# Local attention and feed-forward: columns turned from unshifted rows, norms batch by batch, groups turned singly

## The reference, cut to what matters

```python
def shift_token(t):
    t1, t2 = jnp.split(t, 2, axis=-1)
    t2 = jnp.pad(t2, ((0, 0), (1, 0), (0, 0)))[:, :-1]
    return jnp.concatenate([t1, t2], axis=-1)

def _layer(x, wqkv, qs, ksc, wo, lg, lb, w1, b1, w2, b2):
    h = shift_token(x)
    q, k, v = jnp.split(h @ wqkv, 3, axis=-1)
    q, k = l2norm(q) * qs, l2norm(k) * ksc
    q, k = rotary_xpos(q, k)
    x = x + local_attention(q, k, v) @ wo
    h = shift_token(x)
    h = (h - mu) / jnp.sqrt(var + 1e-05) * lg + lb
    a, g = jnp.split(h @ w1 + b1, 2, axis=-1)
    return x + (a * gelu(g)) @ w2 + b2

for l in range(2): y = _layer(y, ...)     # y = layernorm(x) at first
x = x + y
```

## Time and profile before

| | us |
|---|---|
| median of 3 runs | 4430.23 (4429.78 to 4431.81) |
| the profiled execution | 4434.21 |
| its span in the profile | 4432.4 |
| TensorE busy | 3285.2 (74%) |
| VectorE busy | 3454.3 (78%) |
| ScalarE busy | 2186.3 (49%) |
| GpSimd busy | 2297.1 (52%) |

### The profile page before, as it was taken

One profiled execution on the slowest core, in us unless ns is written; L12 is line 12 of the kernel. 1 busy time (PEld: TensorE's weight loads), 2 busy tenths in 40 slices (PEclk: granted clock), 3 DMA queues, 4 the chain that ended last, 5 costly groups with the idle time before them and its releaser, 6 DMA issues. The chain is left out here.

```text
span 4432.4 us, 114069 instructions
## 1 busy us (share of the span) xinstructions
PE 3285.2 (74%) x45981; PEld 2789.3 (63%) x45981; DVE 3454.3 (78%) x7349; ACT 2186.3 (49%) x5197; POOL 2297.1 (52%) x2836
## 2 busy tenths in 40 slices
PE   5667777777777777777777744439999469977988
PEld 3667777677777777777777744325666347745764
DVE  4699999999999999999999982137888648745873
ACT  3344444444444444444444421115888459826972
POOL 0566767667676676767767660222111058606860
PEclk9888888888988888888888865669999779988999
DMA  2010111101111011110101103110000111101110
GB/s 69 22 42 23 34 33 32 35 23 34 33 34 33 23 38 29 34 33 23 41 26 34 33 22 104 48 31 1 2 2 2 40 39 40 35 18 40 39 37 21
DMA packets 166580, 142.48 MB, mean 32 GB/s; under 512 B 81776, under 2 KB 117691, under 8 KB 165796
## 3 DMA queue, kind: packets, MB, share of 16 engines
q1 hardware_dynamic: 164004, 131.72, 11.1%
q0 software_dynamic: 2048, 3.45, 0.3%
HBM read 96.00 MB, written 14.69 MB: 25 GB/s over the span
## 5 line engine op out<-in xcount | busy, mean ns | idle before, releaser
L1003 DVE TENSOR_REDUCE banks<-a_tmp 128x64 f32<-128x64 f32 (+14 forms) x960 | 669.5, 697 | 33.1
L455 PE MATMUL banks<-a_xseg,a_w_k 128*128 128x128 f32 x2048 | 304.6, 322 | 166.7 <-DVE a_wx L1010 161.9
L455 PEld LDWEIGHTS banks<-a_xseg,a_w_k 128*128 128x128 f32 x2048 | 298.6, 237 | 173.2 <-DVE a_wx L1010 168.0
L455 PE MATMUL banks<-a_xseg,a_w_v 128*128 128x128 f32 x2048 | 305.3, 322 | 117.3 <-DVE a_wx L1010 115.9
L455 PEld LDWEIGHTS banks<-a_xseg,a_w_v 128*128 128x128 f32 x2048 | 299.2, 237 | 122.7 <-DVE a_wx L1010 121.1
L1001 DVE TENSOR_TENSOR a_tmp<-a_w,banks 128x64 f32<-128x64 f32 (+8 forms) x576 | 346.5, 602 | 25.5 <-DVE a_w L1010 0.5
L782 POOL TENSOR_TENSOR a_w<-a_wx,a_a 128x160 f32<-128x160 f32 (+5 forms) x384 | 288.9, 752 | 149.3 <-DVE a_wx L1010 149.2
L782 POOL TENSOR_TENSOR a_wx<-a_w,a_a 128x128 f32<-128x128 f32 (+5 forms) x384 | 263.1, 685 | 157.8 <-DVE a_w L1010 155.1
L528 PE MATMUL banks<-a_wm,a_kt 64*64 64x64 f32 x8192 | 257.1, 221 | 104.5 <-ACT a_wm L659 104.3
L1001 DVE TENSOR_TENSOR a_tmp<-a_wx,banks 128x320 f32<-128x320 f32 (+5 forms) x384 | 315.7, 822 | 14.0 <-DVE a_wx L1010 0.8
L767 POOL TENSOR_TENSOR a_st<-a_st,a_ab 128x512 f32<-128x512 f32 x256 | 326.1, 1274 | 0.0
(11 more groups left out here) (309 smaller groups left out, 8994.1 us busy)
## 6 DMA issues: line engine op xcount, KB each, us to landing
a_ab<-decays SPq DMA_DIRECT2D x512, 128.0 KB, 3.1
d_Vs<-d_V SPq DMA_DIRECT2D x128, 128.0 KB, 2.3
hs<-y SPq DMA_DIRECT2D x16, 256.0 KB
hs<-y SPq DMA_DIRECT2D x16, 254.0 KB
sent<-b_zero SPq DMA_DIRECT2D x1, 2560.0 KB
b_xe<-sent SPq DMA_DIRECT2D x8, 320.0 KB, 3.8
back<-b_eo SPq DMA_DIRECT2D x8, 320.0 KB, 2.5
a_xseg<-xn SPq DMA_DIRECT2D x32, 70.0 KB, 3.0
```

The source lines that it names most:

```text
L455: t = e.matmul(b[:, m * SW:(m + 1) * SW].rearrange("p (b t) -> p b t", b=NB), self.wT[n][:, j, ct * P:(ct + 1) * P], xs[:, :, off:off + SE ...
L1003: e.tensor_reduce(sums[:, t - 1], prod, AX.X, ALU.add).then_inc(*step.at((g, t, "sum")))
```

## The change

The class `Normalised` and its stage are gone. Attention turns its columns from Y, which isn't shifted: `pe_cols` turns four tiles into a bank of the ring, and `act_cols` copies channels 0 to 63 to the same columns of hT and channels 64 to 127 one column further, so that the copy makes the shift. The first column of each batch is zeroed once per layer by a memset. Group 0 is turned ahead of the loop and group n+1 at step 4n of it. No transfers bring Hs for an attention any more; those for the feed-forward part stay.

In layer 0 an `Entrance` norms batch 0 ahead of the attention, and batches 1 to 3 beside it, in five pieces for a batch at steps 0, 1, 2, 3 and 5 of each eight. In `LocalFFN` the norm of batch 0 is followed by the rows of groups 0 and 1; batch 1 follows before the loop, batches 2 and 3 inside it at n = 1 and 3. Group n+2 gets its rows, its transposes and its ScalarE copy inside pass n. The weights of both local layers are loaded ahead of the banded attention.

```diff
             self.batch(e, q, src, ready, b)
     def batch(self, e, q, src, ready, b):
-        gs = slice(b * TPB, (b + 1) * TPB)
         ready(q, b)
-        for g in range(gs.start, gs.stop):
+        self.moments(e, q, src, range(b * TPB, (b + 1) * TPB))
+        self.roots(e, q, b)
+    def moments(self, e, q, src, tiles):
+        for g in tiles:
             e.bn_stats(self.stats[:, g, :], src[:, g, :]).then_inc(*self.s_stats.at(g))
-        for g in range(gs.start, gs.stop):
+        for g in tiles:
             q.wait_ge(self.s_stats, g)
             e.bn_aggr(self.mv[:, g, :], self.stats[:, g, :]).then_inc(*self.s_mv.at(g))
+    def roots(self, e, q, b):
+        gs = slice(b * TPB, (b + 1) * TPB)
         q.wait_ge(self.s_mv, gs.stop - 1)
         e.tensor_scalar(self.var[:, gs], self.mv[:, gs, 1], EPS, None, ALU.add).then_inc(*self.s_root.at((b, "var")))
         q.wait_ge(self.s_root, (b, "var"))
...
-            self.xn = [c.sb(ctx, f"{name}_xn{i}", [P, 4, D]) for i in range(2)]
+        self.xn = [c.sb(ctx, f"{name}_xn{i}", [P, 4, D]) for i in range(2)]
         self.s_row, self.s_full, self.s_done = (c.sem(f"s_cols_{n}") for n in ("row", "turned", "done"))
+    def rows(self, e, q, n):
+        self.norm.ready(q, n // 2)
+        if n >= 2:
+            q.wait_ge(self.s_full, n - 2)
+        for j in range(4):
+            self.norm.apply(e, self.xn[n % 2][:, j, :], self.src, 4 * n + j).then_inc(*self.s_row.at(4 * n + j))
+    def turn(self, e, q, n):
+        bank = self.c.bank(n % 2)
+        if n >= 2:
+            q.wait_ge(self.s_done, n - 2)
+        q.wait_ge(self.s_row, 4 * n + 3)
+        for j in range(4):
+            t = e.transpose(bank[:, j * P:(j + 1) * P], self.xn[n % 2][:, j, :], self.c.ident[:])
+        t.then_inc(*self.s_full.at(n))
+    def empty(self, e, q, n):
+        out = self.dst[:, n * BANK:(n + 1) * BANK]
+        q.wait_ge(self.s_full, n)
+        if self.affine:
+            e.activation(out, self.c.bank(n % 2), ACT.Identity, scale=self.affine[0], bias=self.affine[1]).then_inc(*self.s_done.at(n))
+        else:
+            e.activation(out, self.c.bank(n % 2), ACT.Copy).then_inc(*self.s_done.at(n))
     def vector(self, e, q):
...
-    def vector(self, e, q):
-        self.Hs.zero(e)
-        self.norm.vector(e, q, self.X, lambda q, b: None)
-        for g in range(NTILE):
-            self.norm.ready(q, g // TPB)
+    def apply(self, e, q, tiles):
+        self.norm.ready(q, tiles[0] // TPB)
+        for g in tiles:
             self.norm.apply(e, self.Y[:, g, :], self.X, g).then_inc(*self.s_y.at(g))
-    def sync(self, e, q):
-        for b in range(NB):
-            q.wait_ge(self.s_y, b * TPB + TPB - 1)
-            self.Hs.bring(e, b, (0, "attention"))
+    def first(self, e, q):
+        self.norm.batch(e, q, self.X, lambda q, b: None, 0)
+        self.apply(e, q, range(TPB))
+    def beside(self, e, q, g):
+        b, r = g // TPB + 1, g % TPB
+        if b >= NB:
+            return
+        t, half = b * TPB, TPB // 2
+        if r < 2:
+            self.norm.moments(e, q, self.X, range(t + r * half, t + (r + 1) * half))
+        elif r == 2:
+            self.norm.roots(e, q, b)
+        elif r == 3:
+            self.apply(e, q, range(t, t + half))
+        elif r == 5:
+            self.apply(e, q, range(t + half, t + TPB))
 class LocalAttention:
-    def __init__(self, c, ctx, k, Y, Hs, W, l, cst_dram, hT):
...
                 q.wait_ge(self.s_qk, (g, what[-1]))
             elif what == "o":
                 q.wait_ge(self.s_ot, g)
+            elif what == "cols":
+                q.wait_ge(self.s_cols, (g, 1))
             else:
                 q.wait_ge(self.s_add, g)
         return self.c.bank(5 + n % 3)
...
     def held(self, what, g):
         return self.c.bank(5 + self.slot[what, g] % 3)
+    def pe_cols(self, e, q, n):
+        b = self.take(q, ("cols", n))
+        for j in range(4):
+            if self.entrance:
+                q.wait_ge(self.entrance.s_y, 4 * n + j)
+            t = e.transpose(b[:, j * P:(j + 1) * P], self.Y[:, 4 * n + j, :], self.c.ident[:])
+        t.then_inc(*self.s_colturn.at(n))
     def pe_project(self, e, q, g, which):
+        q.wait_ge(self.s_edge)
         for what in which:
             z = "qkv".index(what)
             b = self.take(q, (what, g))
-            q.wait_ge(self.cols.s_done, g // 4)
+            q.wait_ge(self.s_cols, (g // 4, 1))
             e.matmul(b, self.hT[:, g * P:(g + 1) * P], self.W.wqkv[:, z * INNER:(z + 1) * INNER], start=True,
                      stop=True).then_inc(*self.s_proj.at((g, what)))
...
     def tensor(self, e, q):
         self.W.ready(q)
-        self.cols.tensor(e, q, lambda q, b: (q.wait_ge(self.Hs.s_zero), self.Hs.ready(q, b, (self.l, "attention"))))
+        self.pe_cols(e, q, 0)
         for g in range(3):
             self.pe_project(e, q, g, "qkv")
             if g == 1:
...
                 self.pe_scores(e, q, g)
             if before >= 0:
                 self.pe_turn_out(e, q, before)
+            if g % 4 == 0 and g + 4 < NTILE:
+                self.pe_cols(e, q, g // 4 + 1)
             if coming < NTILE:
                 self.pe_project(e, q, coming, "qk")
             if 0 <= last < NTILE:
...
                 self.pe_project_out(e, q, before)
+    def act_cols(self, e, q, n):
+        half, c0 = D // 2, n * BANK
+        more = BANK - n % 2
+        q.wait_ge(self.s_colturn, n)
+        e.activation(self.hT[0:half, c0:c0 + BANK], self.held("cols", n)[0:half, :], ACT.Copy).then_inc(*self.s_cols.at((n, 0)))
+        e.activation(self.hT[half:P, c0 + 1:c0 + 1 + more], self.held("cols", n)[half:P, 0:more], ACT.Copy).then_inc(*self.s_cols.at((n, 1)))
     def act_project(self, e, q, g):
         raw, sw = self.raw[g % 2], self.sw[g % 2]
...
     def vector(self, e, q):
         hf = DH // 2
         tab, sc = self.tab, self.sc
+        e.memset(self.hT[D // 2:P, 0:NT:T], 0.0).then_inc(*self.s_edge.at())
+        if self.entrance:
+            self.entrance.first(e, q)
+            self.Hs.zero(e)
         self.W.ready(q)
         q.wait_ge(self.l_tab, 1)
         e.tensor_scalar(sc[:, 0, :], sc[:, 0, :], -QK_SCALE, None, ALU.mult).then_inc(*self.s_tab.at("scale"))
...
                 self.dve_divide(e, q, g - 1)
             if g >= 2:
                 self.dve_add(e, q, g - 2)
+            if self.entrance:
+                self.entrance.beside(e, q, g)
...
         t.then_inc(*self.s_down.at(n))
     def tensor(self, e, q):
-        self.cols.tensor(e, q)
-        self.rise(e, q, 0)
-        for n in range(1, NT // BANK):
+        last = NT // BANK - 1
+        self.cols.turn(e, q, 0)
+        self.cols.turn(e, q, 1)
+        for n in range(last + 1):
             self.rise(e, q, n)
-            self.fall(e, q, n - 1)
-        self.fall(e, q, NT // BANK - 1)
+            if n:
+                self.fall(e, q, n - 1)
+            if n + 2 <= last:
+                self.cols.turn(e, q, n + 2)
+        self.fall(e, q, last)
     def scalar(self, e, q):
-        self.cols.scalar(e, q)
+        self.cols.empty(e, q, 0)
+        self.cols.empty(e, q, 1)
         for u in range(NT // BANK * NH):
-            f, b = u % NH, self.c.bank(2 + 2 * (u % 2), 2)
-            w = self.wide(f)
+            n, f = divmod(u, NH)
+            b, w = self.c.bank(2 + 2 * (u % 2), 2), self.wide(f)
             q.wait_ge(self.s_up, u)
             if u >= 2:
                 q.wait_ge(self.s_hid, u - 2)
             e.activation(self.gl[u % 2][0:w, :], b[0:w, BANK:], ACT.Gelu, bias=self.W.b1g[0:w, f:f + 1]).then_inc(*self.s_gelu.at(u))
+            if f == NH - 1 and n + 2 < NT // BANK:
+                self.cols.empty(e, q, n + 2)
     def dve_sum(self, e, q, n):
         g = slice(4 * n, 4 * n + 4)
...
                 q.wait_ge(self.s_down, n - 2)
             e.scalar_tensor_tensor(self.hid[n % 2][0:w, f, :], b[0:w, 0:BANK], self.W.b1a[0:w, f:f + 1], self.gl[u % 2][0:w, :],
                                    ALU.add, ALU.mult).then_inc(*self.s_hid.at(u))
-            if n and f == NH - 1:
-                self.dve_sum(e, q, n - 1)
+            self.beside(e, q, n, f)
         self.dve_sum(e, q, NT // BANK - 1)
+    def brought(self, q, b):
+        self.Hs.ready(q, b, (self.l, "ffn"))
+    def beside(self, e, q, n, f):
+        if f == 0 and n + 2 < NT // BANK:
+            self.cols.rows(e, q, n + 2)
+        batch, half = (n + 3) // 2, TPB // 2
+        if n % 2 and batch < NB:
+            t = batch * TPB
+            if f == 1:
+                self.brought(q, batch)
+                self.norm.moments(e, q, self.Hs.ap, range(t, t + half))
+            elif f == 2:
+                self.norm.moments(e, q, self.Hs.ap, range(t + half, t + TPB))
+                self.norm.roots(e, q, batch)
+        if n and f == NH - 1:
+            self.dve_sum(e, q, n - 1)
     def gpsimd(self, e, q):
         pass
     def sync(self, e, q):
-        q.wait_ge(self.cols.s_row, NTILE - 1)
```

(17 more changed lines are left out.)

## The result

The changed kernel takes 4352.44 us (median of 4 runs, 4347.35 to 4352.57) against 4430.00 for the kernel before (4 runs): a ratio of 0.9821, with a 95% interval from 0.9804 to 0.9838. It is faster by 77.6 us. The forecast was 4307, a gain of 123, with a range up to 4338: the sign is right, and 45 us of the gain are missing.

A forecast was written before the change was run, and what follows sets the result against it. Attention and feed-forward loops were taken as full, the entrances as nearly empty, waiting for shifts. Terms -83.7 - 16.6 - 40.2 + 8.4 + 7.8 = -124.3 gave median 4305.9, stated as 4307 us; own range 4296 to 4316, 8-in-10 range 4293 to 4338.

The forecast's parts named there:

- Norms inside attention loop 0: Batches 1 to 3 normed beside attention 0, in pieces behind VectorE's add: 2.6 us a batch, +7.8, bounds 0 and 20.
- the columns: Seven groups per layer turned and copied inside the attention loops: +4.2 us per layer, bounds 0 and +10.9.
- Rival 2: Attention loop 0: VectorE's roots, perhaps rows, wait for GpSimd instructions to end: +15 us, 4322; with rows +12, 4334; 27%.
- The entrance of attention 0: From the end of banded attention to the first rotation: 10.9 us instead of 94.6, term -83.7.
- that of attention 1: From its stage start to the first rotation, no shift ahead of the tables: 8.7 us against 25.3, term -16.6.
- both feed-forward parts: First rise at 7.9 us instead of 31.9, less costs of cold TensorE and turned groups: term -20.1 twice.
- A step with a group: Sign in the attention loops: steps of 8.32 us, with every fourth, which turns columns, at 8.9.
- A half of 64 rows: ScalarE's column copy in two halves, each priced like a full copy; two back to back take 1.06 us.
- the roots step: Sign in attention 0: the step holding the norm's roots near 9.8 us; 13 or more would mean GpSimd holds VectorE.
- Rival 1: Attention loops: new VectorE pieces and the columns cost their full busy time, +18 us: 4325; 12%.
- rival 3: TensorE's granted clock falls after idle time at the roots and at the entrances, +14 us: 4321; 7%.
- Rivals 4 and 5: Loops at low clock, slower than before, 4560 with half the steps, 2%; no gain at feed-forward entrances, +40 us, 4347, 2%.

The follow-up runs named there:

- second experiment: Changed kernel with GpSimd's six large instructions of a step working on one head instead of all; 0.9702 of the kernel before.
- fifth experiment: Changed kernel with the roots and rows moved in VectorE's order, between rotation product and sum of squares; 0.9751 of the kernel before.

## Why the prediction was wrong

**The step that failed** is the term "Norms inside attention loop 0": +7.8, bounds 0 and 20. The loop lost 57.2 us; 4.4 of it are the columns (as in attention 1), so the norms cost some 52.8, 17.6 a batch for 2.6 (17.3 by the pace against that of the norms ahead). The place of each piece, what is queued behind it and who waits for that were right: with GpSimd out of the way the pieces cost 2.1 a batch (second experiment). Wrong were the durations. I took 2.35 for the roots and 1.05 for four rows from the earlier trace rows, where GpSimd has nothing to do, and put them where it is busy 174.63 of 200 us. The upper bound of 20 had the same fault: "all the busy time" was the busy time of idle surroundings.

**Rival 2 named the mechanism**, with 27%, and missed its size. Its prices come on top of the sum's own 2.6 a batch. For the roots it had 5 longer (measured: 7.4 against 2.35, so 5.1: right), with the sum's 1.5 that is 6.5 a batch; the pace rose by 8.2. What it lacks is about the 2 us that TensorE's low clock adds behind a stall of 5.85 us. For the rows it had four passing in one gap, 2 longer a piece, with the sum's 0.5 that is 4.5 a batch for 7.9. In fact the gap between two GpSimd instructions (0.08, from 3633.36 to 3633.44 and again from 3650.50 to 3650.58) lets one row through, and GpSimd's next instruction holds the one behind it. The four rows from 3647.12 took 0.35, 0.77, 2.50 and 2.06, and the last two ended 0.08 behind GpSimd's two long instructions; a piece was 3.6 or 4.4 longer. With the measured 17.6 a batch in place of 2.6 the sum would have been 4307 + 3 x 15 = 4352, outside even this rival's 4334. The earlier trace rows had what it takes to size it. An estimate from them, with one row to an instruction: three of the short ones of 0.70 and the first long one of 2.5 (3757.24 to 3759.76) give 4.6 a piece, one short one and both long ones (2.5 and 1.90) give 5.1; measured were 4.64 and 5.44.

The prediction says that the trace before has no VectorE instruction with two tensors in SBUF under a running GpSimd instruction. It has one kind, in an earlier stage: the sum of the experts' rows to x (L1349, 128x128) overlapped a `DMA_INDIRECT` of GpSimd in 24 of its 32 executions, and took 343 to 352 ns in all 32. So a GpSimd instruction that issues an indirect transfer didn't hold it. Of GpSimd's tensor instructions, which did hold VectorE here, that stage says nothing.

**What was right.** The entrance of attention 0 (10.55 for 10.9), that of attention 1 (8.9 for 8.7), both feed-forward parts (20.2 and 20.6 for 20.1), and the columns: 4.4 in layer 1 for 4.2, and 4.0 in layer 0, where the kernel with the norms ahead takes 296.5 us from the first rotation to the last tile for 292.5 before. A step with a group is 9.12 us long by ScalarE's exponentials (4103.48 to 4112.60) for 8.9 forecast:

```profile
4103.48 0.40 ACT L2047 ACTIVATE d_S<-d_S,d_low 128x128 f32<-128x128 f32 x1 [0.32 <-DVE d_low L2110]
...
4111.39 0.58 ACT L2001 ACTIVATE d_hT<-banks 64x512 f32<-64x512 f32 x1
4111.99 0.59 ACT L2002 ACTIVATE d_hT<-banks 64x511 f32<-64x511 f32 x1
4112.60 0.40 ACT L2047 ACTIVATE d_S<-d_S,d_low 128x128 f32<-128x128 f32 x1
```

A half of 64 rows does cost what a full copy does. The two follow each other at 0.60, and not at the 0.46 that I had from a pair in one group, so they take 1.2 and not 1.06. That the roots step would show 9.8, or 13 and more under rival 2, was the right test: it shows 14.7.

**Rival 1** (VectorE's order alone) is refuted by the fifth experiment, **rival 3** (the clock) holds in part, as an echo of 2 us behind a long stall; it starts nothing. **Rivals 4 and 5** did not come.

## What to carry to other kernels

A duration belongs to its surroundings. Before a VectorE instruction is moved beside a working GpSimd, ask whether it reads two SBUF tensors or is a copy or tensor_scalar from SBUF to SBUF; if so, price it at one GpSimd instruction for each of the first few, not at its own length. Often nothing has to be given up: the same twelve instructions cost 7.4 us behind the addition and 2.7 just ahead of the result that GpSimd waits for. And when one stage of two alike loses time, compare the two first: here attention 1 was the control, in the trace from the start.

## What the hardware showed

- In the changed kernel a root step on 8 columns takes 0.17 us beside an idle GpSimd and up to 2.21 beside a working one, and each one that waited ended 0.02 or 0.03 us behind a GpSimd instruction. GpSimd's own durations don't change (its addition takes 2361 ns on average beside the pieces and 2365 without), so here VectorE alone pays.
- Moments (L145: 273 to 288 ns beside GpSimd, 274 to 295 alone), sums, fills and reciprocals pass beside GpSimd, and so do additions and products with one operand in PSUM: the mask addition L2108 takes 0.66 to 0.69 us in every step of the loop, and 45 of 61 overlap a GpSimd instruction.
- A row of 128x128 over columns in steps of two is held like any other (762 to 2520 ns).
- With 5.85 us without work up to 3637.42, TensorE had a granted clock of 0.50 in the 4 us from 3638, and of 0.80 in the 4 after those.
